# Decoder layer on one core: the 192 context channels of the cross-attention taken as 128 and 64 rows, and the keys of a sequence computed in one quarter

## The reference

```python
q = (query @ Wq + bq).reshape(B, Nq, H, D).transpose(0, 2, 1, 3)
k = (key_value @ Wk + bk).reshape(B, Nkv, H, D).transpose(0, 2, 1, 3)
v = (key_value @ Wv + bv).reshape(B, Nkv, H, D).transpose(0, 2, 1, 3)
attn = jnp.einsum('bhqd,bhkd->bhqk', q, k) * scale
attn = jax.nn.softmax(jnp.clip(attn, -CLAMP, CLAMP), axis=-1)
x = jnp.einsum('bhqk,bhkd->bqhd', attn, v).reshape(B, Nq, Cq) @ Wo + bo
```

## Time and profile before

| | |
|---|---|
| median of 3 runs | 1531.82 us (1529.16 to 1534.66) |
| profiled execution | 1531.24 us, span 1529.4 us |
| PE / DVE / ACT / POOL busy | 87% / 65% / 38% / 52% of the span |
| keys matmuls, L1732 | 256 records, 93.6 us |
| values matmuls, L1757 | 384 records, 98.5 us |
| `kf` copies, L1291 | 64, 36.7 us |
| context transfers | 32 of 270.8 KB |

### The profile page before, as it was taken

The page is one execution under the profiler, slowest core; times in us unless marked ns, Lnnn a source line. Parts: engine busy times, 40 slices in busy tenths (PEclk is TensorE's granted clock), DMA queues, the critical chain, the costliest instruction groups (busy, mean ns, idle before and its releaser), DMA issues.

```text
span 1529.4 us, 31293 instructions
## 1 busy us (share of the span) xinstructions
PE 1333.5 (87%) x9916; PEld 896.1 (59%) x9917; DVE 998.6 (65%) x2060; ACT 580.3 (38%) x1422; POOL 798.8 (52%) x1143
## 2 busy tenths in 40 slices
PE   3787788788864799999999999999997999999996
PEld 2465455456542466666666666666664566666664
DVE  2688977977872288888888888888885422222221
ACT  1333233233320255555555555555553222221211
POOL 3225524623633556777778877777773422222222
PEclk9999999999977599999999999999998999999998
DMA  4993000000000554555554445555542332322221
GB/s 145 310 317 105 1 1 1 0 0 0 1 0 25 94 102 106 122 121 123 123 123 109 114 121 124 120 119 122 121 119 61 56 49 43 47 44 45 45 45 21
DMA packets 152682, 128.02 MB, mean 84 GB/s; under 512 B 41362, under 2 KB 145442, under 8 KB 152546
## 3 DMA queue, kind: packets, MB, share of 16 engines
q1 hardware_dynamic: 140242, 112.22, 29.4%
q0 software_dynamic: 12304, 14.10, 6.0%
HBM read 36.10 MB, written 44.83 MB: 53 GB/s over the span
## 4 chain that ended last, share of the span: by engine, by line
PE 53%; DVE 7%; issue 3%; ACT 2%; DMA 1%; SPq 0%; POOL 0%; DVEq 0%; ACTq 0%; POOLq 0%
PE bank_st L1937 10%; PE bank_v L1955 6%; PE bank_s L1769 6%; PE bank_v L1757 6%; PE bank_o L1799 4%; PE bank_st L1779 4%; DVE neg_raw L1471 3%; PE bank_m L1732 3%; PE bank_s L1937 3%; PE bank_m L1821 2%; PE bank_st L1788 2%; PE bank_o L1946 2%; DVE bank_st L1482 2%; PE bank_v L1747 1%; ACT heads_t L1331 1%
## 5 line engine op out<-in xcount | busy, mean ns | idle before, releaser
L1471 DVE TENSOR_REDUCE neg_raw<-bank_s 100x2 f32<-100x722 f32 x256 | 229.4, 896 | 31.2 <-PE bank_s L1769 31.0
L1318 ACT ACTIVATE prob<-bank_st 120x400 f32<-120x400 f32 (+1 forms) x384 | 166.2, 514 | 161.1 <-PE bank_st L1788 161.1
L1258 POOL DMA_INDIRECT out<-result,target x57 | 88.3, 1549 | 234.5 <-DVE result L1676 216.4
L1482 DVE TENSOR_SCALAR bank_st<-bank_st 121x1200 f32<-121x1200 f32 x128 | 180.3, 1409 | 2.1 <-PE bank_st L1779 1.5
L753 PE MATMUL bank_l<-q_heads,k 128*100 128x192 f32 (+4 forms) x512 | 121.8, 378 | 63.2 <-DVE attn L567 49.9
L1671 DVE TENSOR_TENSOR hidden<-silu,bank_st 128x512 f32<-128x512 f32 x57 | 39.2, 688 | 194.9 <-PE bank_st L1937 194.9
L1937 PE MATMUL bank_st<-expert_w,rows_t 128*128 x344 | 160.7, 604 | 0.8 <-issue 0.5
L401 ACT ACTIVATE q_heads<-q 32x192 f32<-32x192 f32 (+3 forms) x168 | 62.1, 369 | 224.0 <-DVE q L526 218.4
L753 PEld LDWEIGHTS bank_l<-q_heads,k 128*100 128x100 f32 x512 | 80.4, 175 | 111.8 <-DVE attn L567 41.3
L1769 PE MATMUL bank_s<-k_st,q_st 96*128 96x361 bf16 x512 | 123.2, 322 | 15.5 <-DVE neg_raw L1471 9.8
L1157 POOL TENSOR_TENSOR neg_diag<-xident_b,neg_max 100x400 bf16<-100x400 bf16 x128 | 109.2, 853 | 46.0 <-DVE neg_max L1476 45.4
(11 more groups left out here) (231 smaller groups left out, 2734.6 us busy)
## 6 DMA issues: line engine op xcount, KB each, us to landing
k_st<-k_part SPq DMA_DIRECT2D x384, 90.2 KB
slot_rows<-empty SPq DMA_DIRECT2D x9, 2967.0 KB, 25.8
q_st<-q_part SPq DMA_DIRECT2D x192, 50.0 KB
kv<-in_ctx_t SPq DMA_DIRECT2D x32, 270.8 KB
expert_w<-in_w SPq DMA_DIRECT2D x16, 512.0 KB, 4.1
rows<-slot_rows SPq DMA_DIRECT2D x57, 129.0 KB
residual<-in_w SPq DMA_DIRECT2D x16, 256.0 KB, 4.4
residual<-in_x SPq DMA_DIRECT2D x8, 400.0 KB
```

The costliest lines, as they stand in the source:

```text
L1318: act.activation(prob[0:KEYS[c], t % 2, c], bank_st[0:KEYS[c], c, 0:4 * T], ACT.Exp).then_inc(exp_done, 1)
L1471: dve.tensor_reduce(neg_raw[:, h:h + 2], bank_s[0:T, :, 0:S], AX.X, ALU.max, negate=True).then_inc(max_done, 1)
L1482: dve.tensor_scalar(tile, tile, CLAMP, -CLAMP, ALU.min, ALU.max).then_inc(clipped, 1)
```

## The change

The channels are now split as 128 and 64 rows. The 64 remaining rows are held twice, in partitions 0 to 63 and 64 to 127, of `kv` and of the weights. The keys of both output halves are computed in quarter 2: two matmuls over 128 rows, into `bank_m` and `bank_v`, then two over 64 rows, one in the lower and one in the upper rows of the array. `turn`, which writes `bank_v`, now waits until both halves are copied out. On ACT both copies stand ahead of the exponentials of quarter 2. `values` keeps six matmuls for a sequence, three over 128 rows and three over 64. The transfer of a context grows from 192 to 256 rows of 1444 bytes.

```diff
-            kv = dead.enter_context(nc.sbuf_tensor("kv", [KC, 2, 2, S], F32))
+            kv = dead.enter_context(nc.sbuf_tensor("kv", [128, 2, 2, S], F32))
@@ ACT
-                act.activation(kf[:, c], bank_m[:, 0:S], ACT.Identity, bias=b_k[:, c:c + 1]).then_inc(k_done, 1)
+                act.activation(kf[:, c], (bank_m, bank_v)[c][:, 0:S], ACT.Identity, bias=b_k[:, c:c + 1]).then_inc(k_done, 1)
+                    if more_than(b, 2) and t == 2:
+                        keys(b + 2, 0)
+                        keys(b + 2, 1)
                     exps(4 * b + t, t)
-                    if more_than(b, 2) and t >= 2:
-                        keys(b + 2, t - 2)
@@ PE
-            def keys(b, p, c):
-                if c == 0:
-                    pe.wait_ge(kv_loaded, 16 * (b + 1))
-                    after(pe, x_done, b - 2)
-                after(pe, k_done, CC * b + c)
-                for i in range(2):
-                    mm = pe.matmul(bank_m[:, 0:S], w_k[:, i, c * 128:(c + 1) * 128], kv[:, p, i],
-                                   start=(i == 0), stop=(i == 1))
-                mm.then_inc(k_summed, 1)
+            def keys(b, p):
+                pe.wait_ge(kv_loaded, 16 * (b + 1))
+                after(pe, x_done, b - 2)
+                after(pe, k_done, CC * b)
+                after(pe, v_done, 3 * b)
+                for c, bank in enumerate((bank_m, bank_v)):
+                    pe.matmul(bank[:, 0:S], w_k[:, 0, c * 128:(c + 1) * 128], kv[:, p, 0], start=True, stop=False)
+                for c, bank in enumerate((bank_m, bank_v)):
+                    rest = slice(KR * c, KR * c + KR)
+                    pe.matmul(bank[:, 0:S], w_k[rest, 1, c * 128:(c + 1) * 128], kv[rest, p, 1], start=False,
+                              stop=True).then_inc(k_summed, 1)
             def turn(b):
                 pe.wait_ge(xn_done, b + 1)
-                after(pe, v_done, 3 * b)
+                pe.wait_ge(k_done, CC * (b + 1))
@@ values on PE
-                for i in range(2):
+                for i, rows_in in enumerate((128, KR)):
                     mm = pe.matmul(bank_v[0:KEYS[c], (c % 2) * D:(c % 2 + 1) * D],
-                                   kv[:, p, i, KEY0[c]:KEY0[c] + KEYS[c]], w_v[:, i], start=(i == 0), stop=(i == 1))
+                                   kv[0:rows_in, p, i, KEY0[c]:KEY0[c] + KEYS[c]], w_v[0:rows_in, i], start=(i == 0),
+                                   stop=(i == 1))
@@ body on PE
-                    if more2 and t >= 2:
-                        keys(b + 2, p, t - 2)
+                    if more2 and t == 2:
+                        keys(b + 2, p)
@@ layout
-        return v.reshape(2, KC, -1).transpose(1, 0, 2)
+        return np.stack([v[0:128], np.concatenate([v[128:], v[128:]])], 1)
```

More of the change, by code:

```diff
@@ L37 @@
 S = 361
-KC = 96
+KR = 64
 NH = 16
@@ L839, in stage_attention_experts @@
         w_q = sb("xw_q", [128, CC, D])
-        w_k = sb("xw_k", [KC, 2, D])
-        w_v = sb("xw_v", [KC, 2, D])
+        w_k = sb("xw_k", [128, 2, D])
+        w_v = sb("xw_v", [128, 2, D])
         w_o = sb("xw_o", [128, CC, D])
@@ L1375, in _ @@
                 keys(b, 0)
+                keys(b, 1)
+                keys_high(b, 0)
                 turned(b)
-                keys_high(b, 0)
-                keys(b, 1)
                 keys_high(b, 1)
@@ L1856, in _ @@
             for b in (0, 1):
-                keys(b, b, 0)
+                keys(b, b)
                 turn(b)
-                keys(b, b, 1)
                 queries(b)
@@ L2085, in halves @@
     def halves(v):
-        return v.reshape(2, KC, -1).transpose(1, 0, 2)
+        return np.stack([v[0:128], np.concatenate([v[128:], v[128:]])], 1)
     out.update({
-        "ctx_t": i["ctx_768"].transpose(0, 2, 1), "xq": blocks(by_channel(a["Wq"])),
+        "ctx_t": np.concatenate([i["ctx_768"], i["ctx_768"][:, :, 128:]], 2).transpose(0, 2, 1), "xq": blocks(by_channel(a["Wq"])),
         "xk": halves(by_channel(a["Wk"])), "xv": halves(a["Wv"]), "xo": blocks(a["Wo"]),
```

## The result

The changed kernel takes 1569.28 us (median of 4, 1567.58 to 1572.70) against 1530.51 for the kernel before on the same chip (median of 4): ratio 1.0251, 95% interval 1.0231 to 1.0271. The prediction was 1566, in a range of 1530 to 1582. The difference of the medians is 38.8 us where the sum had 34.7.

The account below looks back on a forecast made before the run. PE looked like the bound (busy 503 of 530 us), DVE close behind, the two taking turns. Lateness of 10.2 us at quarter 0 plus 24.5 for values made 34.7 on the profiled 1531.24: 1566 us, range 1530 to 1582.

Parts of the forecast that it names:

- The keys themselves: Keys in quarter 2: two rounds for the four remainder records, 1.81 us for all keys, 0.61 less than before.
- rival (3): Keys: float32 records must begin in program order, so seven rounds, last copy 0.30 later, 9 us: 1575; chance 0.07.
- The price of a block: Entering and leaving the divided array costs 0.28 us a block, four more blocks a sequence: keys once, values three times.
- Rival (1): Divided rows: no price, so values cost nothing and keys 0.12 less, 7 us: 1538; chance 0.2.
- rival (2): Divided blocks: exposed weight loads add 0.08 us at six sides, 15 us in all: 1581; chance 0.12.
- Quarters 2 and 3: Turn waits for both key copies until K + 3.30; quarter 0's scores then begin 0.78 (even) and 0.57 (odd) late.
- Quarter 0: Second scores 0.43 us late in even and 0.25 in odd sequences; mean 0.34 over 30 sequences: 10.2 us.
- Values: Divided values in quarters 0 and 1: 0.56 plus 0.28 less 0.05 slack, 0.79 us a sequence, 31 times: 24.5 us.
- Other parts: Larger context transfer hidden; before the first sequence, larger transfers and changed waits: nothing taken, 1 us for the range.
- Rival (4): PE's work alone sets the pace: saved key time and waits come back, 23 us faster, 1508; chance 0.11.
- the forecast: Whole kernel: the main case, slower, alone 1550 to 1578 us; chance 0.5.

Follow-up runs that it names:

- experiment 1: Changed kernel with all values matmuls over 128 rows (upper weight rows zero), keys as changed: 1544.88 us, ratio 1.0077.
- 8: Changed kernel with both 64-row key remainders in the lower rows of the array, one after the other, not paired: 1580.42 us, ratio 1.0301.
- 9: Changed kernel with quarter 0's two 128-row values matmuls first and the two 64-row ones behind them, one block instead of two: 1557.97 us, ratio 1.0173.
- 2: Changed kernel with the turn moved on PE from quarter 2 to quarter 3, ahead of the shift, ACT's order kept: 1570.01 us, ratio 1.0242.
- 3: Changed kernel with the turn moved to quarter 3 and, on ACT, the key copies behind the exponentials of quarter 2: 1554.06 us, ratio 1.0137.
- experiment 4: Changed kernel with values over 128 rows (zero padded), the turn in quarter 3 and ACT's key copies behind the exponentials: 1536.71 us, ratio 1.0020.
- 6: Kernel before with only the new layout: 256-row transfer, weights zero padded to 128 rows, old order, no 64-row matmul: 1529.81 us, ratio 0.9980.
- 7: Kernel before with the new layout and only the values' remainders over 64 rows, keys zero padded in the old order: 1548.38 us, ratio 1.0097.
- 10: Changed kernel with quarter 0's values matmuls reordered into one block, the turn in quarter 3 and ACT's key copies behind the exponentials: 1544.03 us, ratio 1.0084.

## Why the prediction came out right, step by step

**The keys themselves and the divided array.** Two rounds, as said, with pairs of records started 7 ns apart; rival (3), seven rounds, is refuted. The price of a block was taken as 0.28 from a block of column groups; it measured 0.30 for the keys, 0.28 for the last values, 0.67 for two values blocks in quarter 0, where 0.56 was said; the 0.10 behind the first full-row record between the two was the part that no column block had shown. At the entry the single records of the earlier trace rows are 0.137 apart where their neighbours are 0.045 apart, the same 0.09 as for rows. Rival (1), no price, falls with experiment 1; rival (2), 0.08 more at every side, falls with these sizes. The block's 0.30 is the same whether the 64 rows are paired or not (8), and falls away when two are joined (9). Whether PE drains there or weight loads are no longer hidden was not separated. The Trainium skill, TensorEngine Tiling (Array Packing), Key Properties, says that a change of tiling mode drains TensorE; the measured 0.093 at each side agrees with it, but does not single it out. The Trainium skill, TensorE: Matmul & The Clock Gate, Part 3, has matmuls start in strict program order; the start of the second bank's first record at 843.83, 0.40 ahead of the first bank's second record, does not show that order between the two matmuls.

**Quarters 2 and 3.** Said and measured from K: the turn 3.30 and 3.37, scores 3.47 and 3.57, shift 6.32 and 6.46, scores of quarter 0 7.70 and 7.84. Each step is late by 0.07 to 0.14. That begins inside the block: its second round starts at 844.23 - 842.52 = 1.71 where 1.63 was said, since the rounds are 0.41 apart and not 0.30. The 0.44 between two `kf` was read from a `kf` and a `qf`; two `kf` start 0.46 apart. The turn waited 0.57, where some 0.7 was said. Experiments 2 and 3 show both halves of the mechanism: the turn behind the copies holds the scores, and once it is gone the copies ahead of the exponentials hold the transposed scores.

**Quarter 0.** Late by 0.43 even and 0.25 odd were said; 0.40 (9.77 - 9.37) and 0.23 (9.44 - 9.21) measured. Over 29 sequences experiment 1 keeps 594.4 - 584.1 = 10.3, where 10.2 was said for 30; but 2.1 of it are the first two of them, and the other 27 lose 0.30 each where 0.34 was said, so the near equality of the totals is in part luck. The 0.15 for DVE was a guess that happened to fit; experiment 4 shows what it is worth when `neg_max` falls worse: 9.35 - 8.78 = 0.57.

**Values.** 24.5 us were said and experiment 1 gave back 24.4. By sequence it is 0.80 (23.2/29) for 0.79. The two parts were off in opposite senses: 0.67 for 0.56 in quarter 0, and in quarter 1, where the block costs the 0.28 as said, 0.13 is left of the 0.80 where 0.23 was said. In the total, 3.7 lie in the start and -1.5 in the last two sequences, where 1.6 and nothing were said. The agreement to 0.1 is luck; the mechanism is not. The term is also no constant: 0.61 a sequence in the order of before (7), where the odd sequence has a wait to give.

**Other parts.** The wider transfer costs nothing (6), as said. The mis-sized term is the start: "nothing taken, 1 us for the range". It measured 7.0, of which the sum had 0.34 + 2 x 0.79 = 1.9 under quarter 0 and values; 5.1 stand against the nothing. PE at the first turn and at the keys of the second sequence:

```profile
507.01 0.57 PE L1743 MATMUL bank_v<-xident,xxn 100*128 100x100 f32 x2 [1.19 <-ACT kf L1291]
518.98 1.54 PE L1733 MATMUL bank_m<-kv,xw_k 128*128 128x361 f32 x2 [0.57 <-ACT xval L1336]
```

Before the first sequence nothing else is there to run while the copies are made, so waits that are hidden later stand open: 1.19 for the second `kf`, and a new one of 0.57 for the copy of the values, since the keys now write `bank_v` too. Between first keys and first scores this is 24.6 us (526.18 - 501.57), against 22.1 (523.93 - 501.80) before: +2.5. From first keys to the keys of the second sequence it is 17.4 (518.98 - 501.57), against 14.9 (516.67 - 501.80) before and 16.3 in experiment 1 (518.26 - 501.98), all at a granted clock of 0.50: 1.4 for the keys with their waits and 1.1 for the divided values. From there to the first scores nothing is lost. The next 2.7 lie between the first scores and the next keys (544.84 - 526.18 = 18.66 for 539.91 - 523.93 = 15.98), and the last 1.85 behind those, as in each of the next two sequences. The windows of the start, before (length, then busy us of PE, PEld, DVE, ACT and POOL, granted clock, DMA share, GB/s):

```profile
532.00:537.00 5.00, 4.96 (x51) 3.00 (x51) 2.76 (x3) 1.85 (x5) 2.80 (x6) 0.81 0.57 113
537.00:542.00 5.00, 4.91 (x54) 2.86 (x52) 3.78 (x6) 2.56 (x7) 1.30 (x2) 1.00 0.39 85
```

and after:

```profile
532.00:537.00 5.00, 5.00 (x12) 1.98 (x11) 1.92 (x3) 0.67 (x3) 4.68 (x9) 0.50 0.71 99
537.00:542.00 5.00, 5.00 (x47) 3.20 (x46) 3.39 (x4) 1.23 (x4) 0.53 (x1) 0.63 0.19 38
542.00:547.00 5.00, 4.91 (x52) 2.60 (x51) 3.32 (x5) 2.00 (x5) 1.37 (x2) 1.00 0.28 74
```

The granted clock returns from the 1.2 GHz level to the 2.4 GHz level later. A share of 0.81 in 5 us at these two levels is 1.9 us at the lower one, one of 0.63 is 3.7, so it is back at 533.9 before and at 540.7 after, 6.8 us later. In between PE has the eight values records of the first attention sequence: from first start to shift they take 4.41 (536.23 - 531.82) where they took 3.41 before (532.54 - 529.13). Experiment 9, with the two blocks joined, tells what they do. Its first scores come as late (526.15 - 501.52 = 24.63), with a granted clock of 0.84 and 0.50 in the two windows ahead, for 0.84 and 0.51 after. But then the same records take 2.96 (534.75 - 531.79), and the clock is back within the window from 532:

```profile
532.00:537.00 5.00, 4.70 (x25) 2.49 (x24) 2.79 (x4) 1.85 (x5) 4.68 (x9) 0.82 0.71 98
```

Its start is 58.3 long, 3.0 less than the 61.3 of the changed kernel, and 2.6 of these lie between the first scores and the next keys; 10 against 3, the same edit in the other order, gives 57.6 for 60.7, though there the granted clock ahead is not the same. So the stretch at the lower clock is longer with two divided blocks than with one. Why the clock rises when it does was not tried. Each start is read from one execution, and the granted clock ahead of the first scores differs between kernels where the edit gives no reason for it: the start of 6, in before's order, is 52.1, 2.2 below before, with a full clock from 508 to 521. So the 7.0 is good to some 2 us, and by the medians and their interval (35.4 to 41.5 us in all) to some 3.

**Sum.** Said 34.7; measured 33.5 in the 29 sequences, 7.0 in the start, -1.5 in the last two, -0.2 in the rest: 38.8. The sum put 29 x (0.34 + 0.79) = 32.8 on the 29 sequences, 1.9 on the start and nothing on the last two, which have no keys and no values to compute. So the 29 are off by 0.7 (two early sequences at 1.85, the others at 1.10 for 1.13), and what was missing is the start. Why the last two sequences are 1.5 shorter is open; they are 44.2 to 44.6 in after, 7, 8 and 9, where the values are divided, but 45.1 to 45.2 in 2, 3 and 10, where they are too, and 45.2 to 45.8 in the others. Rival (4), faster, needed the maximum of quarter 3 to begin no later than K + 3.04; its scores alone came at K + 3.57. The chances of the prediction do not quite add up: the forecast, (2), (3) and half of (1) give slower 0.79, where 0.75 was written.

## What to carry to other kernels

Before matmuls are cut to fit fewer rows, count how often the array changes between whole and divided: here each block of half-array matmuls cost about 0.3 us whatever it held. For the values, padding with zeros or putting divided matmuls together was faster than 64 rows each time; for the keys, where two remainders could run side by side, the block took 2.12 us where padding took 2.43, and the kernel hardly felt the difference. None of the kernels with divided matmuls was faster than the one before. When two results are produced together and a shared bank passes to the next user, put the copies that free it, and what waits for them, behind the work that others wait for; mending PE's order alone won nothing here, mending PE's and ACT's together 15 us. A change's price depends on the slack that it meets (0.61 or 0.80 for the same values matmuls), and the first items of a pipeline, where nothing covers a wait and the clock may be at its lower level, need a term of their own.

## What the runs showed of the hardware

- Two float32 matmuls over 64 rows in the two halves of the array, into different banks, run side by side: their records start in pairs 6 or 7 ns apart, the two rounds 0.41 apart, where one record over 128 rows takes 0.303.
- A block of half-array matmuls between whole ones cost 0.093 us at the entry, 0.10 behind its first record, 0.093 at the exit and nothing more for the records behind them: 0.28 to 0.30 in all. Between two blocks of the values 0.10 more was lost behind the first full-row record. This held for 2 or 4 records one behind another and for two pairs.
- A DVE instruction on 400 elements took 0.17 to 1.35 us; in the rows where it was long it ended within 0.03 us of a POOL tensor operation beside it. Others ran beside POOL and stayed short.
- With the half-array values at the start in one block, the granted clock was 0.82 in the window from 532 us and 1.00 in the next; with them in two, 0.50, the 1.2 GHz level, and 0.63.
